# Codebook and ids loaded to one partition, the first row retimed, and column groups of 512, 324 and 324

## The reference, cut to what matters

```python
lora_delta = lora_B @ lora_A * 2
cb = codebook / max(max|codebook|, 1e-8)          # 64 values, not sorted
normalized = ((weight + lora_delta).reshape(1024, 8, 128)) / exp(scale_log)
idx = searchsorted((cb[:-1] + cb[1:]) * 0.5, normalized, side='left')
w_eff = (cb[idx] * scale) + lora_delta
```

## Time and profile before

| | us |
|---|---|
| median of 3 runs | 912.48 |
| lowest and highest | 910.99 and 912.91 |
| the profiled execution | 910.95 |
| its span | 909.1 |
| TensorE (PE) busy in it | 902.2 (99%) |
| VectorE (DVE), ScalarE (ACT), GpSimd (POOL) busy | 616.5, 313.2, 144.0 |

### The profile page before, as it was taken

How to read it: one execution, slowest core, us unless ns; L and a number is a source line. 1 busy time by engine, 2 the same in 40 slices (tenths; PEclk the granted TensorE clock), 3 DMA queues, 4 the chain that set the end, 5 groups by cost and what they waited for, 6 DMA issues and landing times.

```text
span 909.1 us, 13369 instructions
## 1 busy us (share of the span) xinstructions
PE 902.2 (99%) x4670; PEld 787.0 (87%) x4670; DVE 616.5 (68%) x1312; ACT 313.2 (34%) x503; POOL 144.0 (16%) x298
## 2 busy tenths in 40 slices
PE   8999999999999999999999999999999999999998
PEld 7999998888998888888888888888888888888886
DVE  6889899865587968976456566566566566566563
ACT  5678778411324433231322222222222222222220
POOL 0100010111001001414213113113113113113110
PEclk9999999999999999999999999999999999999999
DMA  8523330765412033556887887887888887887875
GB/s 340 208 76 122 119 125 24 259 211 166 142 50 94 4 135 94 216 211 225 280 277 258 284 274 262 282 272 263 285 272 266 280 265 270 286 270 263 287 225 184
DMA packets 60540, 191.51 MB, mean 211 GB/s; under 512 B 7965, under 2 KB 10678, under 8 KB 58554
## 3 DMA queue, kind: packets, MB, share of 16 engines
q1 hardware_dynamic: 49610, 159.02, 50.5%
q0 software_dynamic: 10432, 31.35, 11.6%
q10 hardware_dynamic: 432, 0.30, 0.1%
HBM read 158.93 MB, written 32.23 MB: 210 GB/s over the span
## 4 chain that ended last, share of the span: by engine, by line
PE 95%; DMA 4%; SPq 0%; ACT 0%; DVE 0%; issue 0%
PE bank L857 28%; PE bank L519 15%; PE bank L520 15%; PE bank L521 15%; PE bank L840 5%; PE bank L831 5%; DMA t_lo<-t_scratch 3%; PE bank L665 2%; PE bank L905 2%; PE bank L931 2%; PE bank L932 2%; PE bank L933 2%; DMA m_raw<-m1t 1%; PE bank L774 1%; PE bank L580 1%; PE bank L537 0%
## 5 line engine op out<-in xcount | busy, mean ns | idle before, releaser
L857 PE MATMUL bank<-g_hi,xs 128*128 128x512 f32 x448 | 145.2, 395 | 0.0
L857 PE MATMUL bank<-t_hi,xs 128*128 128x512 f32 x336 | 113.3, 396 | 0.3 <-DMA t_lo<-t_scratch 0.2
L490 POOL DMA_DIRECT2D p1sel<-p_scratch x128 | 65.3, 510 | 278.9 <-issue 278.8
L857 PEld LDWEIGHTS bank<-g_hi,xs 128*128 128x128 f32 x448 | 83.3, 188 | 16.3
L857 PE MATMUL bank<-g_lo,xs 128*128 128x512 f32 x224 | 88.3, 394 | 0.0
L977 ACT ACTIVATE xs<-x_raw 128x1024 fp32r<-128x1024 f32 x60 | 61.9, 1056 | 76.1 <-PE bank L857 55.7
L1309 DVE TENSOR_TENSOR xs<-x_raw,xs 128x1024 fp32r<-128x1024 f32 x60 | 75.4, 1279 | 12.0 <-ACT xs L977 11.5
L519 PE MATMUL bank<-gx,xs 128*128 128x304 f32 x256 | 77.5, 303 | 0.0
L521 PE MATMUL bank<-gx,xs 128*128 128x304 f32 x256 | 77.5, 303 | 0.0
L520 PE MATMUL bank<-gx,xs 128*128 128x304 f32 x256 | 77.3, 302 | 0.0
L857 PEld LDWEIGHTS bank<-t_hi,xs 128*128 128x128 f32 x336 | 62.1, 188 | 15.2 <-DMA t_lo<-t_scratch 2.9
(11 more groups left out here) (325 smaller groups left out, 2060.9 us busy)
## 6 DMA issues: line engine op xcount, KB each, us to landing
t_hi<-t_scratch SPq DMA_DIRECT2D x82, 512.0 KB, 4.7
t_lo<-t_scratch SPq DMA_DIRECT2D x82, 512.0 KB, 6.2
x_raw<-xq SPq DMA_DIRECT2D x16, 1024.0 KB, 6.8
out<-ost SPq DMA_DIRECT2D x63, 256.0 KB, 4.3
p1sel<-p_scratch POOLq DMA_DIRECT2D x64, 192.0 KB, 4.4
w_raw<-wall SPq DMA_DIRECT2D x16, 512.0 KB, 4.4
w<-e_scratch SPq DMA_DIRECT2D x6, 1024.0 KB, 5.1
ea<-e_scratch POOLq DMA_DIRECT2D x8, 644.0 KB, 4.5
```

The lines of the kernel that those rows point to most:

```text
L490: pool.dma_start(f(p1sel[b][STK * s:STK * s + STK, cs]), p1_dram[bass.ds(i * STK, STK), cs]).then_inc(sems[b], 16)
L857: mm = nc.tensor.matmul(bk[j][:], l[:, c, :], m[:, c, :], start=first and c + k == 0, stop=c + k == KH + 1, skip_group_check=True)
```

## The change

The codebook and the ids go to one partition, issued by GpSimd ahead of everything else it does. All codebook steps up to the reach flags work on one partition. VectorE waits for the codebook first and does the whole normalisation, the midpoints and two of five tree levels before and beside the first splits. `row0_low(1)` moves ahead of chunk 2. The three small TensorE steps move to (0, 5), (0, 7) and (1, 2). Six steps of the exponential move behind the ranking, and VectorE's split of weight block 2 behind the spread codebook. The column groups change width.

```diff
-A_COLS = [(0, 388), (388, 388), (776, 384)]
+A_COLS = [(0, 512), (512, 324), (836, 324)]
-CB_AT = {(1, 0): 0, (1, 2): 1, (1, 6): 2}
+CB_AT = {(0, 5): 0, (0, 7): 1, (1, 2): 2}
-        cb = row("cb", [P, LV])
+        cb = row("cb", [1, LV])
...
-            sp.dma_start(idraw[:], ids_b).then_inc(ld_ids, 16)
...
         def _(pool):
+            pool.dma_start(cb[:], cbook_r).then_inc(ld_cb, 16)
+            pool.dma_start(idraw[:], ids_r).then_inc(ld_ids, 16)
             pool.wait_ge(ld_ids, 16)
...
-                if c == 0:
-                    row0_low(0)
-                if c > 1:
+                if c < 2:
+                    row0_low(c)
+                elif c > 2:
                     row0_low(c - 1)
...
-            act.dma_start(cb[:], cbook_b).then_inc(ld_cb, 16)
...
+            v.wait_ge(ld_cb, 16)
+            mag = vcomp[0:1, :]
+            link(nc.vector.tensor_scalar(mag, cb[:], -1.0, None, ALU.mult))
...   (max, reduce, floor, reciprocal, scale, midpoint sum, times 0.5: 8 linked steps in all)
             v.wait_ge(ws_hi, 1)
             lo_of(w_lo[0][:, 0:2, :], w_raw[0][:, 0:2, :], w_hi[0][:, 0:2, :]).then_inc(ws_lo, 1)
+            for h in (1, 2):
+                midpoints(h, 0)
+                link(midpoints(h, 1))
             for c in range(KC):
                 m1_split(c)
                 if c == 1:
                     w_split(0)
-                if c > 1:
-                    codebook_scale(c - 2)
             w_split(1)
...
+            for h in range(3, 6):
+                midpoints(h, 0)
+                link(scale_step(2 * h - 5))
+                midpoints(h, 1)
+                link(scale_step(2 * h - 4))
+            link(nc.vector.tensor_tensor(reach[:], tt_[:, 0:LV], tt_[:, 1:LV + 1], ALU.is_lt))
+            nc.vector.reduce_sum(rs2[0][0:1, 0:1], reach[:], AX_X).then_inc(cols_ok, 1)
+            link(scale_step(7))
+            nc.vector.tensor_copy(cnt[0:1, 0:1], rs2[0][0:1, 0:1])
+            v.wait_ge(cols_mm, 1)
+            nc.vector.tensor_copy(cols[:, 0:3], bk[3][0:LV, 0:3]).then_inc(cols_ok, 1)
...   (the split of the low-rank factors, the rank step, scale_step 8 to 13)
             nc.vector.tensor_copy(valid[:], bk[3][:, 192:256]).then_inc(comp_ok, 1)
+            w_split(2)
             v.wait_ge(comp_ok, 1)
```

More of the change, by code:

```diff
@@ L199, in build @@
         val0 = small("val0", [P, 1])
-        idc = small("idc", [P, T // SEQ], I32)
+        idc = small("idc", [1, T // SEQ], I32)
         bv = small("bv", [P, 12])
@@ L214, in build @@
         tr_at = [tr]
-        cb = row("cb", [P, LV])
-        tt_ = row("tt_", [P, LV + 1])
-        reach = row("reach", [P, LV])
+        cb = row("cb", [1, LV])
+        tt_ = row("tt_", [1, LV + 1])
+        reach = row("reach", [1, LV])
         cols = row("cols", [LV, 4])
@@ L221, in build @@
         valid = row("valid", [P, LV])
-        idraw = row("idraw", [P, T // SEQ], I32)
-        idf = row("idf", [P, T // SEQ])
+        idraw = row("idraw", [1, T // SEQ], I32)
+        idf = row("idf", [1, T // SEQ])
         one1 = row("one1", [P, 1])
@@ L286, in build @@
         st_o = [sem(f"st_o{j}") for j in range(4)]
-        cbook_b = cbook.rearrange("(a n) -> a n", a=1).to_broadcast([P, LV])
-        ids_b = ids.rearrange("(a n) -> a n", a=1).to_broadcast([P, T // SEQ])
+        cbook_r = cbook.rearrange("(a n) -> a n", a=1)
+        ids_r = ids.rearrange("(a n) -> a n", a=1)
         chunked = lambda ap: ap.rearrange("(c p) n -> p c n", p=P)
@@ L1350, in _, with midpoints @@
             link(nc.vector.memset(tt_[:, LV:LV + 1], 4.0))
[L1351 to L1364, removed]
+            v.wait_ge(ld_cb, 16)
+            mag = vcomp[0:1, :]
+            link(nc.vector.tensor_scalar(mag, cb[:], -1.0, None, ALU.mult))
+            link(nc.vector.tensor_tensor(mag, mag, cb[:], ALU.max))
+            link(nc.vector.reduce_max(val0[0:1, :], mag, AX_X))
+            link(nc.vector.tensor_scalar(val0[0:1, :], val0[0:1, :], 1e-8, None, ALU.max))
+            link(nc.vector.reciprocal(val0[0:1, :], val0[0:1, :]))
+            link(nc.vector.tensor_scalar(cb[:], cb[:], val0[0:1, 0:1], None, ALU.mult))
+            link(nc.vector.tensor_tensor(tt_[:, 1:LV], cb[:, 0:LV - 1], cb[:, 1:LV], ALU.add))
+            link(nc.vector.tensor_scalar(tt_[:, 1:LV], tt_[:, 1:LV], 0.5, None, ALU.mult))
+            def midpoints(h, side):
+                half = 1 << h
+                view = tt_[:, 0:LV].rearrange("p (b w) -> p b w", w=2 * half)
+                mid = view[:, :, half:half + 1].to_broadcast([1, LV // (2 * half), half - 1])
+                part = view[:, :, half + 1:2 * half] if side else view[:, :, 1:half]
+                return nc.vector.tensor_tensor(part, part, mid, ALU.max if side else ALU.min)
             v.wait_ge(ws_hi, 1)
             lo_of(w_lo[0][:, 0:2, :], w_raw[0][:, 0:2, :], w_hi[0][:, 0:2, :]).then_inc(ws_lo, 1)
+            for h in (1, 2):
+                midpoints(h, 0)
+                link(midpoints(h, 1))
             for c in range(KC):
@@ L1371, in _ @@
                     w_split(0)
-                if c > 1:
-                    codebook_scale(c - 2)
             w_split(1)
             v.wait_ge(ld_pk, 16)
-            nc.vector.tensor_tensor(tt_[:, 1:LV], cb[:, 0:LV - 1], cb[:, 1:LV], ALU.add)
             link(scale_step(0))
[L1378 to L1393, removed]
+            for h in range(3, 6):
[9 more added lines that the diff above has]
+            nc.vector.tensor_copy(cols[:, 0:3], bk[3][0:LV, 0:3]).then_inc(cols_ok, 1)
             v.wait_ge(la_hi_s, 1)
             lo_of(la_lo[:], la_raw[:], la_hi[:]).then_inc(la_lo_s, 1)
[L1396 to L1399, removed]
             v.wait_ge(cols_mm, 2)
@@ L1402, in _ @@
             nc.vector.tensor_scalar(selm[:], iota, cols[:, 3:4], cols[:, 2:3], ALU.is_equal, ALU.mult).then_inc(cols_ok, 1)
-            w_split(2)
+            v.wait_ge(la_hi_s, 2)
+            lo_of(lb_hl[64:P, :], lb_raw[64:P, :], lb_hl[64:P, :]).then_inc(la_lo_s, 1)
+            for k in range(8, 14):
+                link(scale_step(k))
             v.wait_ge(cols_mm, 3)
```

## The result

| | before | after |
|---|---|---|
| median of 20 executions each, us | 911.39 | 913.71 |
| lowest and highest | 910.0 and 913.39 | 911.77 and 915.12 |
| the profiled execution, its span | 910.95, 909.1 | 914.93, 913.2 |

The ratio is 1.0024, with a 95% interval of 1.0017 to 1.0031: the kernel is 2.3 us slower by the medians, where I forecast 2.4 us faster.

What follows compares the result with a forecast made beforehand. TensorE was taken to bound the kernel, busy 902.2 of 909.1 us. Gains of 1.5 + 0.2 + 0.6 + 0.1 = 2.4 us took 912.48 to 910.1 us, range 908.7 to 912.3.

Steps and rivals of the forecast that it cites:

- the early codebook chain: Row 0, VectorE's codebook steps ahead of its first split: cost nothing if the codebook lands by 4.3 us; 3.6 expected.
- The rival of the late codebook: Row 0: codebook lands at 8.1 us, VectorE delays row 1 to 24.3; 0.9 us slower, 913.4 us; chance 0.07.
- Forecast 20.95: Start of row 1 after the change, in us, in place of 22.50.
- Term 1: Row 0: transfers 1.2 us earlier without the codebook's broadcast, plus the new order; row 1 starts 1.5 us sooner.
- The first rival: Early transfers: the dip in DMA rate is not the broadcast's; row 0 gains only 0.3, total 911.3 us; chance 0.16.
- Terms 2 and 4: Row 1's two small-step waits go, 0.2 us gained; row 3's identity no longer crosses a border, 0.1 us gained.
- Term 3: Rows 1 to 8: matmul widths 512, 324, 324 make each triple 0.003 us shorter; 0.6 us gained.
- the second rival: Matmul widths: width has no price, or 512 is dear on these operands; gain 1.8 us, 910.7 us; chance 0.20.

Runs made afterwards that it cites:

- e9: Kernel after, with SP and ScalarE waiting for the codebook before their first loads, so GpSimd's load meets empty queues; one execution, 914.37 us.
- e10: Kernel after with the codebook issued by SP ahead of chunk 0, the same kernel as e7 measured again; 909.38 to 911.23 us before, ratio 0.9981.
- e2: Kernel after with VectorE's codebook wait and steps moved back between and behind the splits; 909.89 us to 911.51 before, ratio 0.9994.
- e3: Kernel after with 16 more matmuls on zeros to keep TensorE busy in row 0; 911.91 us to 911.62 before, ratio 1.0003.
- e1: Kernel before with only the one-partition codebook and ids loads issued by GpSimd, codebook steps at old places; 910.22 us to 911.62, ratio 0.9987.
- e4: Kernel before with only the new column widths 512, 324 and 324; 911.65 us to 911.23 before, ratio 1.0014.
- e11: e7 with the old column widths 388, 388 and 384; 909.27 us to 911.23 for the kernel before, ratio 0.9979.
- e7: Kernel after with the codebook issued by SP ahead of chunk 0; 909.77 us to 911.51 before, ratio 0.9997, one of 11 executions at 921.0.
- e6: Kernel after with the first weight quarter issued by SP ahead of chunk 0, not by ScalarE; 912.73 us to 911.62 before, ratio 1.0007.
- e5: Kernel after with the codebook issued by ScalarE ahead of the first weight quarter; 912.55 us to 911.62 before, ratio 1.0015.
- e8: e7 with 20 matmuls on zeros at the start in place of 15; 909.6 us to 911.51 for the kernel before, ratio 0.9990.

## Why the prediction was wrong

**The step that failed** is in the early codebook chain: "its small transfers land 2.7 us after issue, so 3.6 us, with 0.7 us to spare". The 2.7 us are a median over 64 loads of 25.5 KB later in the kernel. At the start it took 5.9 us, and the issue came at 1.42, not 0.9. The landing at 7.38 us is 3.1 us past the point of 4.3 us that I had named myself. e9 shows that the figure was ample for empty queues (1.9 us) and wrong for this place; e10 that with a landing at 2.2 us the cost is nothing, as I had it; e2 that without the wait in front the late landing costs nothing either. I had excused the 7.2 us of the old codebook load as those of 128 pieces. They were the nearest row in time and place, and they were nearer to the truth.

**A second cost stood in no sum.** The rival of the late codebook has row 1 at the first split plus 14.2 us. That sum holds at full clock: e3 has its split at 8.92 and row 1 at 23.15, for 23.12. In the kernel after, with the split at 9.19, it gives 23.4, and row 1 is at 25.09: TensorE waits 1.53 us, does three matmuls and stands still again, the granted clock falls to 0.50 at about 8.4 us, and until about 15.3 us the triples take nearly twice their time. I read the clock of the windows before (1.00) and never asked what it would do when TensorE stood still. In the profiled executions it costs about as much as the late split. That the late split brings it on is shown by e2: the same first wait (1.41 us), but TensorE goes on at 8.15 us, and the clock stays at 1.00.

**Row 0, by its parts.** Forecast 20.95. e10 has 21.24, 0.3 later. The late landing adds 1.9 (e3, 23.15), the clock 1.9 (25.09), of which 0.27 is still landing. Together 4.1 us.

**Term 1, the transfers**, was right in mechanism and size: 1.2 us forecast for chunk 3, 1.29 measured in the kernel after (12.28 to 10.99) and 1.12 in e1; row 1 gains 1.1 us in e1 and 1.26 in e10, where I had 1.5. Of these 1.5 us 0.3 were the new order's. No run changes the order alone; e2 and e10, which have it, gain 1.2 and 1.3 us at row 1 to e1's 1.1, so 0.1 to 0.2 us can be seen of it. The first rival (the dip belongs to something else) is out. In the dip the DMA engines' share is 0.59 and 0.81: they were not full of small pieces, they stood idle for a part of the time. The Trainium skill (DMA: Bandwidth & Descriptors, Queues, rings and completion order) lets an engine take turns between its queues by the packet. My estimate from it was under 0.1 us for the broadcast's pieces; e1's 1.1 us speak against that estimate. The same page (Anatomy of one DMA, the path of GpSimd) gives about 2.0 us as the fixed cost of such a load. e9's 1.9 us agree; the 5.9 us of the kernel after do not, and the measurement decides.

**Terms 2 and 4** were right: 0.3 us forecast, 0.30 measured from row 1 to the second product (112.31 to 112.01), with the widths worth nothing (e4: 112.39). The other runs agree: 112.29 in e1, with the old places, and 112.01 to 112.13 in all ten kernels with the new ones, e11 with the old widths among them (112.13). None of TensorE's waits in the kernel after lies at the three moved steps or at `delta(0)`.

**Term 3, the widths**, was mis-sized: 0.6 us forecast, zero measured; the second rival was true. The kernel after has a full row in 12.82 us, the kernel before in 12.81:
```profile
83.94 0.40 PE L520 MATMUL bank<-m_hi,w_hi 128*128 128x512 f32 x1
...
96.76 0.39 PE L520 MATMUL bank<-m_hi,w_hi 128*128 128x512 f32 x1
```
A 512-wide matmul on these operands takes 0.233 us (89.30 - 83.94, over 23), on those of the second product 0.2269. I had taken a middle between a row with the right width on other operands and one that was dearer; the dearer one (0.231) was the nearer. The 324-wide ones take 0.149 (54.44 - 49.82, over 31), where I had interpolated 0.1484. The Trainium skill (TensorE: Matmul & The Clock Gate, Back-to-back issue gap) gives an isolated matmul a fixed 2.5 ns above its columns, and so no price for where 1160 columns are cut. The runs agree with that outcome, though not with the 2.5 ns: 324 wide has 14 ns above its columns at 2.4 GHz, 512 wide 20.

**The sum again.** 4.1 us at row 1 and 0.6 of term 3 are 4.7 us, which is the way from the forecast's 2.4 us gained to the 2.3 us lost at the second product. The rival of the late codebook was what happened, at a chance of 0.07, but it was only 0.9 us slower than before, not 2.3: it took a later landing (8.1 for 7.38) and no clock. That its 913.4 us stand so near to the measured 913.7 is luck. It was counted from the 912.48 of three runs, and the kernel before has a median of 911.39 in 20.

**The version that beats both.** e10, or e11 with the old widths: one row on SP's queue, ahead of chunk 0, everything else as changed; 0.9981 and 0.9979 of the kernel before. With e7's lone execution at 921.0 its interval takes in no change, so the gain of 0.2% rests on e10 and e11.

## What to carry to other kernels

A wait that is moved in front of everything needs the landing time of its transfer at that place, with the streams that run beside it; a median from elsewhere in the kernel is no bound. Where the sum has TensorE standing still early on, price the clock too: in the profiled executions here it about doubled the cost of the wait. And when a change with several parts loses, take single parts out before giving it up: another queue for one load (e10) turned the loss into a gain, and the wait put back (e2) made the loss go.

## What the runs showed of the hardware

- A 256-byte load by GpSimd took 1.9 us with nothing beside it (e9) and 5.6 to 5.9 us as the first of two beside SP's stream of 4640-byte pieces (kernel after, e1, e2, e3, e6). The ids' load, where it was GpSimd's only one, took 4.0 to 5.4 us (e5, e7, e8, e10, e11). By SP or ScalarE, issued at 0.88 or 0.89 us ahead of all else on its queue, such a load took 1.3 us (e5, e7, e10).
- The weight quarter (128 KB) took 5.0 us when it was issued at 0.89 beside SP's chunk 0 at 0.88 (kernel after), 5.5 when it was issued at 1.45 (e5), and 3.1 when chunk 0 was issued at 1.29, after it (e10); 3.0 on SP's own queue ahead of chunk 0 (e6). Half a us of issue order moved its landing by up to 2 us.
- The granted clock fell to 0.50 at about 8.4 us in the kernel after, when TensorE had waited 1.53 us, done three matmuls (to 8.28) and was idle again; in e5 at about 8.75, behind a wait of 2.49 us; in e6, with waits of 0.80, 2.14 and 1.08 us and three matmuls between one and the next, only at about 11.7; in e9 at about 10.3, behind 3.26 us. It did not fall in e3, where most of the waits were filled, nor in e2 with one wait of 1.41 us, nor in the kernel before with waits of 0.73 and 1.21 us.
